# A decoder layer on one core: cross-attention and feed-forward in one block, the first x prepared in the last slot, most of the last output projection behind the last values

## The reference

```python
x = x + attn(layernorm(x))                  # 16 heads, linear attention, Wo, gate, norm
x = x + xattn(layernorm(x), ctx_1024)       # 16 heads of 32, softmax over 750 keys, w_proj
x = x + ffn(layernorm(x))

def bitlinear(x, w):                        # x to 8-bit steps by row, w to -1, 0, 1
    return act_quant(x) @ weight_quant(w).T
ffn(x) = bitlinear(silu(bitlinear(x, w_gate)) * bitlinear(x, w_up), w_down)   # inner 2048
```

## Time and profile before

| | us |
|---|---|
| median of 3 runs | 1323.49 (1322.82 to 1323.86) |
| the profiled execution | 1325.15 |
| its span | 1323.5 |

### The profile page before, as it was taken

The page is one execution under the profiler, slowest core; times in us unless marked ns, Lnnn a source line. Parts: engine busy times, 40 slices in busy tenths (PEclk is TensorE's granted clock), DMA queues, the critical chain, the costliest instruction groups (busy, mean ns, idle before and its releaser), DMA issues. The chain is left out here.

```text
span 1323.5 us, 25163 instructions
## 1 busy us (share of the span) xinstructions
PE 1188.4 (90%) x9482; PEld 909.1 (69%) x9482; DVE 813.7 (61%) x1492; ACT 589.0 (45%) x967; POOL 542.0 (41%) x436
## 2 busy tenths in 40 slices
PE   4899989996668999999999999999999986599997
PEld 4687877884557887887878787878787764244443
DVE  6766646665335666565666565666664784477774
ACT  3322222223214544444445444444454673377775
POOL 0011101115103666575665665656656101455541
PEclk9999999998679999999999999999999988799998
DMA  5222242223441234335253343352533690111211
GB/s 165 90 77 89 77 143 89 89 76 125 119 106 50 74 84 127 94 97 132 52 143 86 83 128 97 90 137 50 135 85 80 195 296 16 40 63 56 71 63 40
DMA packets 76138, 129.43 MB, mean 98 GB/s; under 512 B 18764, under 2 KB 35276, under 8 KB 76027
## 3 DMA queue, kind: packets, MB, share of 16 engines
q1 hardware_dynamic: 63267, 104.28, 28.8%
q0 software_dynamic: 11680, 21.81, 5.3%
q10 hardware_dynamic: 1104, 2.15, 0.5%
HBM read 68.96 MB, written 11.22 MB: 61 GB/s over the span
## 5 line engine op out<-in xcount | busy, mean ns | idle before, releaser
L1293 DVE TENSOR_REDUCE xa_m_part<-xa_psM 112x1 f32<-112x376 f32 x512 | 266.4, 544 | 230.2 <-PE xa_psM L1472 228.0
L1188 ACT ACTIVATE space<-xa_psS 125x448 f32<-125x448 f32 x384 | 208.2, 544 | 181.3 <-PE xa_psS L1456 179.8
L1096 POOL TENSOR_TENSOR xa_p_sum<-xa_p_sum,space 125x896 f32<-125x896 f32 x112 | 238.1, 2125 | 97.9 <-ACT space L1188 93.5
L1472 PE MATMUL xa_psM<-xa_k,xa_q 104*112 104x376 f32 x512 | 161.1, 353 | 9.3 <-DVE xa_m_part L1293 4.2
L1456 PE MATMUL xa_psS<-xa_q,xa_k 104*125 104x224 f32 x768 | 146.1, 272 | 0.5 <-ACT space L1188 0.5
L1456 PEld LDWEIGHTS xa_psS<-xa_q,xa_k 104*125 104x125 f32 x768 | 138.4, 188 | 3.4 <-issue 0.7
L1472 PEld LDWEIGHTS xa_psM<-xa_k,xa_q 104*112 104x112 f32 x512 | 87.7, 177 | 28.9 <-DVE xa_m_part L1293 8.5
L1079 POOL TENSOR_SCALAR xa_oT_hi<-xa_o_f 128x224 fp32r<-128x224 f32 x32 | 25.2, 789 | 199.3 <-DVE xa_o_f L1309 199.3
L1496 PE MATMUL xa_psO<-space,cv 125*32 125x224 f32 x1536 | 95.8, 361 | 1.0 <-ACT space L1188 1.0
L1442 PE MATMUL xa_psR<-xa_cT_hi,w_lo 128*128 128x376 f32 x256 | 92.0, 359 | 0.0
L1442 PE MATMUL xa_psR<-xa_cT_hi,w_hi 128*128 128x376 f32 x256 | 87.0, 340 | 1.7 <-DVE xa_cT_lo L1283 1.7
(11 more groups left out here) (216 smaller groups left out, 2698.1 us busy)
## 6 DMA issues: line engine op xcount, KB each, us to landing
xa_k<-xa_k_st SPq DMA_DIRECT2D x378, 94.0 KB, 2.2
xa_q<-xa_q_st SPq DMA_DIRECT2D x192, 56.0 KB, 2.0
cv<-in_ctx_dram POOLq DMA_DIRECT2D x7, 1500.0 KB, 23.0
cv<-in_L_ffn_w_gate_dram SPq DMA_DIRECT2D x14, 512.0 KB, 4.7
cv<-in_L_ffn_w_down_dram SPq DMA_DIRECT2D x10, 512.0 KB, 7.3
cv<-in_L_ffn_w_up_dram SPq DMA_DIRECT2D x9, 512.0 KB, 6.2
sa_x_raw<-in_x_dram SPq DMA_DIRECT2D x8, 448.0 KB, 7.9
sa_rows<-in_x_dram SPq DMA_DIRECT2D x8, 448.0 KB, 4.0
```

Source lines behind the costliest of these rows:

```text
L1096: nc.gpsimd.tensor_tensor(p_sum[:], before, tile, ALU.add).then_inc(p_summed, 1)
L1188: nc.scalar.activation(pT[:, (s + i) % 2, j], psS[0:KB, (HG * i + j) % NB, 0:2 * N], ACT.Exp).then_inc(exp_done, 1)
L1293: V.tensor_reduce(m_part[:, t, jj, seg:seg + 1], psM[0:T, seg, 0:SEG], AX.X, ALU.max).then_inc(mx_read, 1)
L1472: M.matmul(psM[0:T, seg, 0:SEG], q4[0:ROWS, g, jj, t * T:(t + 1) * T], k4[0:ROWS, g % 2, jj, seg * SEG:(seg + 1) * SEG], start=True, stop= ...
```

## The change

`ternary_ffn` no longer opens a block. It returns its programs for the five engines in pieces, and `cross_attention` calls these pieces in its own block, so the two stages share one block and the meeting of all engines between them is gone. The feed-forward's tiles take places in memory that cross-attention has used: x_raw and xq_T lie in the tile of the key sums, xn, xm and xq in the key staging, h in the packed keys, gate in the packed queries, hm, hq, hq_T, x_res and y in the context's tile; its PSUM tiles are the banks of psS, psM, psO and psR, one each as before. Its own constants are gone but for one of 128x1.

In the order of the engines:

- SP loads x of tile 0 behind the residual of the last batch and ahead of the loads of weight units 18 to 23, once the key sums of batch 7 and the first two stores of x2 allow it. x of tile 1 follows unit 23. The rest of x2 is waited for in two steps (7 batches, then 8, since only tiles 12 and 13 hold rows of the last batch).
- DVE takes the statistics of tile 0 in beat 7 of the last slot and its scale in beat 11, ahead of the last `divide`. Behind it come the statistics of tile 1, `hidden(0, 0)` and `hidden(0, 1)`, then the two residual additions, then the scale of tile 1.
- POOL prepares x of tile 0 ahead of the last `split_heads`, x of tile 1 behind it, and stores the last batch of x2 only then.
- PE makes no output projection in beats 9 and 10. Behind the last `attend` it makes 9 matmuls of Y0, turns x of tile 0, 9 matmuls of Y1, `gate_up(0, 0)`, the last 3 + 3 of Y0 and Y1, and `gate_up(0, 1)` onward.

```diff
-    OUTPUT_AT = {9: 0, 10: 1}
+    FIRST_X_AT, SCALE_X_AT = 7, 11
...
         @block.sync
...
+            ffn_first_x, ffn_rest = ffn_sync(sp)
+            ffn_first_x()
             for unit in range(18, UNITS_W):
                 load_ffn(unit)
+            ffn_rest()
...
         @block.gpsimd
...
+            ffn_prepare, ffn_rest = ffn_gpsimd(pool)
+            ffn_prepare(0)
             split_heads(B - 1, NG - 1)
+            ffn_prepare(1)
             store(B - 1)
+            ffn_rest()
...
         @block.vector
...
+                        if (b, s, k) == (B - 1, NG - 1, FIRST_X_AT):
+                            ffn_statistics(0)
+                        if (b, s, k) == (B - 1, NG - 1, SCALE_X_AT):
+                            ffn_scale_first()
             divide(B - 1, NG - 1)
+            ffn_statistics(1)
+            for c in range(2):
+                ffn_hidden(0, c)
             for what in ("Y0", "Y1"):
                 take(what, B - 1)
+            ffn_second_x()
+            ffn_rest()
...
         @block.tensor
...
-                        if (b, s) == (B - 1, NG - 1) and k in OUTPUT_AT:
-                            last_output(OUTPUT_AT[k], range(0, KT - 1))
+            ffn_turn_x, ffn_gate_up, ffn_rest = ffn_tensor(pe)
+            last_output(0, range(0, KT - 1))
+            ffn_turn_x(0)
+            last_output(1, range(0, KT - 1))
+            ffn_gate_up(0, 0)
             for t in range(NT):
                 last_output(t, range(KT - 1, KT))
+            ffn_rest()
```

In `ternary_ffn` the new pieces of SP, which replace `load_x(0)`, `load_x(1)` and one wait for all stores; the pieces of the other engines hold the statements they held before:

```diff
+        def first_x():
+            sp.wait_ge(places["sums_read"], places["sums_read_all"])
+            sp.wait_ge(x2_stored, 2 * DMA)
             load_x(0)
+        def rest():
             load_x(1)
-            sp.wait_ge(x2_stored, x2.shape[0] * DMA)
-            with sp.Fori(0, TILES - 2) as i:
+            sp.wait_ge(x2_stored, (x2.shape[0] - 1) * DMA)
+            sp.wait_ge(places["weights_read"], places["weights_read_all"])
+            with sp.Fori(0, WHOLE - 2) as i:
                 load_x(i + 2)
                 load_residual(i)
+            sp.wait_ge(x2_stored, x2.shape[0] * DMA)
+            for i in range(WHOLE, TILES):
+                load_x(i)
+                load_residual(i - 2)
```

More of the change, by code:

```diff
@@ L785, in cross_attention @@
+def cross_attention(nc, sems, x1, ctx_rows, k_rows, q_rows, x2, shared, ffn_weights, w_abs, w_deq, out):
     B, N, _ = x1.shape
@@ L892, in cross_attention @@
         c_space = sb("c_space", [P, 2 * KT * S])
-        k_st = sb("k_st", [P, 2, 2 * SEG], F32R)
-        k4 = sb("k4", [P, 2, HG, 2 * SEG], F32R)
-        q_st = sb("q_st", [P, NG, 2, N], F32R)
-        q4 = sb("q4", [P, NG, HG, N], F32R)
+        with ExitStack() as over:
+            k_st, k4, q_st, q4 = (over.enter_context(nc.sbuf_tensor("xa_" + n, shape, F32R)) for n, shape in (
+                ("k_st", [P, 2, 2 * SEG]), ("k4", [P, 2, HG, 2 * SEG]), ("q_st", [P, NG, 2, N]), ("q4", [P, NG, HG, N])))
+        k_st_space = sb("k_st_space", [P, 2 * 2 * SEG])
+        k4_space = sb("k4_space", [P, 2 * HG * 2 * SEG])
+        q_st_space = sb("q_st_space", [P, NG * 2 * N])
+        q4_space = sb("q4_space", [P, NG * HG * N])
         xn_all = sb("xn", [P, NT, D])
@@ L915, in cross_attention @@
         f_raw = ([shared["cv"][:, B % 2, n * WC:(n + 1) * WC] for n in range(3)]
-                 + [q_st[:].rearrange("p g a n -> p (g a n)").bitcast(F32)[:, 0:WC], xn_all[:].rearrange("p t d -> p (t d)")]
+                 + [q_st_space[:, 0:WC], xn_all[:].rearrange("p t d -> p (t d)")]
                  + [c_space[:, n * WC:(n + 1) * WC] for n in range(2 * KT * S // WC)])
         place = lambda n, half: shared["w_all"][:, half, n].bitcast(BF16)
-        p_sum = sb("p_sum", [KB, HG, N])
+        sum_space = sb("sum_space", [P, HG * N])
+        p_sum = sum_space[0:KB].rearrange("p (j n) -> p j n", j=HG)
+        ffn_eps = sb("ffn_eps", [P, 1])
         den = sb("den", [P, N])
@@ L961, in cross_attention @@
         ROWS_IN = DMA * 3
+        ffn_places = {"ident": ident_b, "magic": magic, "eps_half": ffn_eps, "sums": sum_space, "keys": k_st_space,
+                      "packed_k": k4_space, "packed_q": q4_space, "context": c_space, "banks": (psS, psM, psO, psR),
+                      "sums_read": den_full, "sums_read_all": NG * (B - 1),
+                      "outputs_read": [(read[bank_of[what, B - 1]], use_of[what, B - 1]) for what in ("Y0", "Y1")],
+                      "weights_read": f_tern_ready, "weights_read_all": UNITS_W}
+        turned = [[place(n, half) for half in range(2)] for n in range(3)]
+        ffn_sync, ffn_gpsimd, ffn_scalar, ffn_vector, ffn_tensor = ternary_ffn(
+            nc, sems, ctx, ffn_places, x2, stored, I, turned, w_deq, out)
         block = ctx.enter_context(nc.Block())
@@ L1056, in _ @@
                                     pattern=[[1, P]], channel_multiplier=-1).then_inc(const_made, 1)
-            pool.wait_ge(const_made, 4)
+            nc.gpsimd.memset(ffn_eps[:], -0.5).then_inc(const_made, 1)
+            pool.wait_ge(const_made, 5)
             def clear_shift(b, s):
@@ L1221, in _ @@
                                     round_weight(unit)
+            ffn_scalar(act)()
         @block.vector
@@ L1553, in _ @@
                             do(*part)
-                        if (b, s) == (B - 1, NG - 1) and k in OUTPUT_AT:
-                            last_output(OUTPUT_AT[k], range(0, KT - 1))
+            ffn_turn_x, ffn_gate_up, ffn_rest = ffn_tensor(pe)
[3 more added lines that the diff above has]
+            ffn_gate_up(0, 0)
             for t in range(NT):
                 last_output(t, range(KT - 1, KT))
-        return stored, [[place(n, half) for half in range(2)] for n in range(3)]
@@ L1957, in decoder_layer @@
                            shared, ahead)
-            stored, turned = cross_attention(nc, sems, x1, context, k_rows, q_rows, x2, shared, (w_gate, w_up, w_down), w_abs, w_deq)
-            ternary_ffn(nc, sems, x2, stored, w_gate.shape[0], turned, w_deq, out)
+            cross_attention(nc, sems, x1, context, k_rows, q_rows, x2, shared, (w_gate, w_up, w_down), w_abs, w_deq, out)
 _INS = ['x', 'ctx_1024', 'L0_attn_Wq', 'L0_attn_Wk', 'L0_attn_Wv', 'L0_attn_Wo', 'L0_attn_G1', 'L0_attn_G2',
```

626 lines of the change are left out of this document (308 added, 318 removed).

## The result

The changed kernel takes 1300.85 us in the median of four executions (1298.67 to 1303.71), the kernel before 1323.67 (1322.82 to 1324.19, four executions): a ratio of 0.984 with a 95% interval of 0.9817 to 0.9862, so 22.8 us faster. The prediction was 1304.0 in a range of 1300.5 to 1309.5.

What follows compares the result with a forecast made beforehand. It took the serial chain between cross-attention's last slot and the feed-forward loop as the bound, with PE nearly idle there. Seam gain 22.2 less 2.7 for the clock gives 19.5, so 1323.49 becomes 1304.0 us; range 1300.5 to 1309.5.

Steps and rivals of the forecast that it cites:

- seam shorter by: Between last cross-attention slot and feed-forward loop: 22.2 us gained up to `round_hidden`, less 2.7 for the clock, 19.5 net.
- That is 3.9 us, none of it off the path.: Last slot's values: without the 18 projection matmuls ahead of the last logits they start 3.9 us earlier, all counted as gain.
- The clock: PE's 4.5 us pause before the second turned x drops it to 1.2 GHz, costing 2.7 us, bounds 0 and 4.
- the clock stays: Rival at PE's pause before the second turned x: 2.4 GHz holds, nothing given back, 1301.3 us; 15%.
- The rival of an earlier fall: PE's clock falls already around the first turned x, slowing Y1 and gate products; 1305.5 to 1308 us; 25%.
- SP: Load of x ahead of the weight loads delays weights 0.5 to 1 us; cost taken as 0, bound 1 us.
- x of tile 0 was not late: Rival at the first x's load: it queues behind weights and arrives after beat 7; 1305 to 1314 us; 4%.
- The rival of the grown loop: Feed-forward passes lengthen because tiles lie elsewhere; gain gone only from 1.7 us each; 2% for same time as before.

Runs made afterwards that it cites:

- e6: Kernel before with only the 18 projection matmuls moved from beats 9 and 10 to behind the last values; median 1318.88 us, ratio 0.9973.
- e3: Changed kernel with the 18 projection matmuls put back in beats 9 and 10 of the last slot; median 1304.20 us, ratio 0.9861.
- e5: Kernel before with only the shared block, first load of x still waiting for all stores; median 1321.51 us, ratio 0.9994.
- e4: Kernel before with the shared block and x of tile 0 loaded ahead of units 18 to 23; median 1316.93 us, ratio 0.9952.
- e7: Changed kernel with the first x prepared behind the last slot instead of within it; median 1315.22 us, ratio 0.9942.
- e2: Changed kernel plus 18 matmuls nobody reads, filling PE's pause before the second turned x; median 1302.62 us, ratio 0.9859.
- e9: Changed kernel plus matmuls nobody reads: 18 ahead of the second turned x, 12 in PE's pause at the end; median 1298.04 us, ratio 0.9819.
- e0: Changed kernel unaltered, run once more to see what repeats; median 1300.03 us, ratio 0.9838.
- e1: Changed kernel with DVE making the second x's scale ahead of the second hidden and the residual additions; median 1298.39 us, ratio 0.9812.
- e8: Changed kernel with the second x's scale made early and 12 matmuls nobody reads in PE's pause at the end; median 1298.11 us, ratio 0.9818.

## Why the prediction was right, and where it was not

**The sum, step by step.** The prediction wrote its times on the axis of the trace of before; the second values of the last slot start 1.27 us earlier in after (1102.70 instead of 1103.97), so that much is taken off first.

| step | predicted, less 1.27 | trace of after |
|---|---|---|
| last values start | 1105.9 | 1105.89 |
| statistics of tile 0 | 1101.8 | 1101.69 |
| first x turned | 1110.6 | 1110.49 |
| first gate product | 1113.3 | 1112.87 |
| `gate_up(0, 1)` | 1116.5 | 1116.01 |
| residual additions | 1120.5 | 1120.06 |
| second x, its largest value | 1121.9 | 1121.25 |
| second x turned | 1126.2 | 1125.57 |
| `round_hidden` | 1127.0 | 1126.71 |
| seam shorter by | 22.2 - 2.7 = 19.5 | 20.2 |

No step is off by more than 0.7. Following each engine's new list with durations from rows of before was enough, because nearly every operation of the seam has a row there.

**What it got wrong inside.** "That is 3.9 us, none of it off the path." The size was right (3.96 in e6), the statement that none of it lies off the path was not: within the whole change the move is worth 1.4 by the seams and 0.9 without the clock (e3). The total did not suffer, since the sum was made on PE's list, from the turned x on, and the 18 matmuls were counted in that list. Had the parts been added up as single gains, 3.9 would have been too much by 2.5 to 3. The parts as the seams give them, each on top of the one before it: one block 1.2 (e5); the load that no longer waits for the store 5.7 (e4); PE's, DVE's and POOL's order 2.6 (e7); the first x inside the slot 10.7 (after). They add up to 20.2 because each is the difference of two seams, and another order of the steps would share it out otherwise. The course of the clock is in them too. The upper level at the last six matmuls, which e5 had and e4 had not, moves 1.0 from the second part to the first: without it they are 0.2, with at most 0.4 for the meeting, and 6.7. Of the last part 8.7 are the later x and 2.1 the clock of e7.

**The clock.** It was taken as 2.7 with bounds 0 and 4; filling the pause gives back 2.3 (e2 and e9) against after and 2.5 against e0. The prediction's four rows are met: turning 0.6 (0.61), gate product 3.5 (3.59), silu 1.6 late (1.67), the next product slower for a part (2.33). Of the rivals "the clock stays" falls: it fell behind the pause in after, and in e0 too, whose stretch 1124 to 1126 has 0.50. The rival of an earlier fall falls as well: the two gate products take 1.90 each, and the stretch around the turned x has 1.00:

```profile
1110.00:1112.00 2.00, 1.51 (x10) 1.22 (x11) 0.45 (x2) 1.06 (x2) 1.70 (x3) 1.00 0.00 0
```

**The other terms.** SP: the weights behind the new load were issued later (1076.02 instead of 1073.90), more than the 0.5 to 1 us predicted:

```profile
1076.02 10.09 SPq L1410 DMA_DIRECT2D xa_c_space<-in_L_ffn_w_down_dram  x5
```

The cost is 0 as taken, since nothing ahead of the seam waited for them and the seam itself begins behind it. x of tile 0 was not late. The loop's pass is 12.17 us instead of 12.16 in the mean, over ten passes 0.2 us. That is not the new places: e6, with the places of before, has 12.17, and e0, the changed kernel, 12.16. The rival of the grown loop falls.

**The median.** It is 3.1 us below the forecast. Of these 0.7 are the seam (20.2 instead of 19.5). The profiled execution itself took 1303.71, and the four executions of after have mean granted clocks of 0.970 and 0.969 (1303.71 and 1302.25 us) and of 0.975 and 0.974 (1299.45 and 1298.67 us). So where the clock is lower in the mean, the time is longer, and the rest of the 3.1 is as large as this scatter. At which places the quicker ones kept their clock, their times don't tell; that stays open.

That the median lies within the range is in part luck. It is 0.35 us above the lower end, and the same kernel's median in e0, 1300.03, is 0.5 below that end with the same seam. It lies outside the forecast's own 1302 to 1306 too, and closest to the 1301.3 of the rival in which the clock stays, which the traces rule out. The prediction was right in what happens at the seam; how far the executions scatter ahead of it and at the end it left out.

## What to carry to other kernels

At a seam between two stages, look for what the second stage could do before the first is finished: here preparing its first tile and loading it early made 16 of 20 us, and the meeting of the engines nearly nothing. Follow the longest list of an engine through the new order instead of adding up single gains; a move that is worth 4.0 us alone was worth 0.9 in company by the trace. And look at the clock of both traces before you put a difference of seams down to the edit: here it moved 1.0 us from one step to another. And when an order leaves PE idle for some microseconds, ask which dependent work comes right behind: a pause is not free even where PE is not late.

## What the runs showed of the hardware

**The same pause may or may not cost the clock.** Three times the same instructions had the same idle time ahead of them and another clock behind it: 2.42 us was followed by 0.50 in e1 and by 1.00 in e8; 2.60 by 0.50 in after and 2.59 by 1.00 in e0; and behind 3.80 us the last six matmuls began at 0.50 in before and e4, and at 1.00 in e5, where the fall came 1 to 2 us later. The pause of 4.2 us was followed by 0.50 in every trace that has it (after, e0, e3, e7). What ran ahead of the pause was the same both times, so something decides that the profile's rows do not show. The Trainium skill, "TensorE: Matmul & The Clock Gate", Part 1, has the rule that idling lowers the clock; the traces agree for 4.2 us, and between 2.4 and 2.6 us they show both outcomes.

**The same program scatters by 8 us, not by 1.** The first executions of the kernel before lay within 1.4 us. In three later comparisons its medians were 1322.99, 1322.39 and 1322.07 us over 9, 26 and 8 executions, with extremes of 1318.06 and 1326.62. The second values of the last slot, ahead of which PE and ACT have unchanged code, moved by up to 6.8 us from trace to trace. An experiment that is to resolve 2 us needs a distance inside the trace, which here repeated to 0.2 us (48.76 and 48.93; 46.44 and 46.48) where the clock took the same course.
